# A wait for the landing of the third gather ahead, in the edge stage of a graph-attention and mixture-of-experts kernel

## The chip, the core and the metric

The kernel runs on one core of a Trainium2 chip. The metric is the device time of one execution in microseconds (us), lower is better. A core has TensorE (PE, its weight loads are listed apart as PEld), VectorE (DVE), ScalarE (ACT), GpSimd (POOL) and SyncE (SP), which run their own instruction streams and meet at semaphores, and 16 DMA engines that move data between the core's memory and HBM.

## The reference, cut to what matters

The program is a graph layer followed by an expert layer. The change touches the edge part of the graph layer alone:

```python
feat_all = einsum('ni,rhid->rnhd', layernorm(x), conv_weights)      # 8 relations, 4 heads of 64
feat_src_e = feat_all[edge_type, edge_src]                          # one row per edge, 120000 edges
feat_dst_e = feat_all[edge_type, edge_dst]
el = sum(feat_src_e * attn_l[edge_type], -1); er = sum(feat_dst_e * attn_r[edge_type], -1)
e = leaky_relu(el + er, 0.2)
alpha = softmax of e over the edges of one destination node
h = segment_sum(alpha[..., None] * feat_src_e, edge_dst, 3750)      # 3750 nodes x 256
x = x + h + h_bias
x = x + top2_of_8_experts_ffn(layernorm(x))
```

All of it is float32.

## The kernel before, in words

There are three stages, one after the other. `node_stage` normalizes the 3750 node rows, multiplies them with the weights of all relations and stores `feats` in HBM: a row of `FW` = 260 words (256 features and 4 left logits) for each node and relation. `edge_stage` walks over the edges. `route_expert_stage` picks two experts for each node and computes them.

The edges are sorted by destination. 256 consecutive edges are a block of two units of 128 edges (one edge to a partition); a pair is a block together with one tile of 128 destination nodes, and there are 498 pairs. They are taken in 32 groups (`SIZES`: 8 pairs, then 30 groups of 16, then 10). A full group has `GU` = 32 units. The rows of `feats` that a group's edges read are fetched by the 32 gathers of line 798: each is one indirect DMA issued on POOL, which reads an index from each of 128 partitions and brings 128 rows of 260 words (133 KB) into `gath[:, r, u]`. There are `GBUFS` = 3 buffers `r`, taken in turn by the groups, and 996 gathers in all.

What sets the order is written out by hand: every engine has a function `period(g, r, n)`, run in a loop of three groups per turn by `each_period` (line 732 is its loop). In the words of one group `g`:

* POOL (`gather_features`, from line 786): waits until the index columns of its group are there (`idx_ready`), and for each quad `j` of four units until the buffer is free. A buffer is free quad by quad as PE finishes the sums of the group three before (`sum_ready`, value `freed(g, j)`). The waits go through `wait_apart` (lines 158 and 159), an instruction of its own that waits and then counts up an unused semaphore. In the program a wait stands once per four gathers, and the four gathers follow it without a wait. The gathers of groups 0 to 2 wait for nothing.
* DVE: scales the gathered rows by alpha (line 905), adds PE's sums to `acc` (line 914), computes the softmax shifts, and at the end of `period(g)` the logits of the next group (`logits`, line 838), which is the first reader of the gathered rows of group `g + 1`. It waits for one semaphore of the buffer, `gath_in[r]`, to reach the count of all gathers so far into this buffer (`landed`). A gather adds 16 to it when its data has landed.
* ACT: builds one-hot matrices of destinations (lines 1035, 1038), copies their transposes (`hotT`, line 1045), takes the exponentials (lines 1073 to 1075) and scales two quads of a group (line 1063).
* PE: transposes the one-hots (line 1113), looks up the right logits (line 1138), and sums the scaled rows (line 1154).
* SP: loads the edge records (line 183) four groups ahead, and at the end, when all gathers have landed, loads the node rows (line 784).

In the program gathers run ahead of their use: while PE sums the first quads of group `g`, POOL gathers group `g + 3`, and the logits that come next are those of group `g + 1`.

Of the kernel before, what the change touches and what calls it, by code (L numbers as in the profile page):

```python
# [44 lines left out]
BLK = 2  # L45
# [3 lines left out]
GB = 16  # L49
GU = GB * BLK  # L50
assert GU * HEADS == P
SIZES = [8] + [GB] * ((PAIRS - 18) // GB) + [10]
SHORT = GB - SIZES[0]
# [7 lines left out]
GBUFS = 3  # L61
# [93 lines left out]
def wait_apart(pool, sem, value, carrier):  # L155


    pool.wait_ge(sem, value)
    pool.sem_inc(carrier, 1)
# [14 lines left out]
def load_records(nc, sp, sb, edges, meta, g, landed, of=range(GB)):  # L174

    edge_rows = edges.rearrange("t h c e -> (t h) (c e)")
    for b in of:
        if b % 4 == 0:
            starts = nc.values_load_multi_w_load_instructions(
                sb["pair_row"][0:1, bass.ds(g, 1), b:b + 4].rearrange("a g b -> a (g b)"), engines=(mybir.EngineType.SP,),  # L180
                min_val=0, max_val=(CHUNK_ROWS - BLK) * HEADS)[1]
        at = starts[b % 4]
        sp.dma_start(meta[b * BLK * HEADS:(b + 1) * BLK * HEADS], edge_rows[bass.ds(at, BLK * HEADS), :]).then_inc(landed, 16)
# [441 lines left out]
def edge_stage(nc, sb, edges, feats, xb, wr, br):  # L625
# [6 lines left out]
    with ExitStack() as ctx:  # L632
# [6 lines left out]
        def sem(name):  # L639
            return ctx.enter_context(nc.semaphore(name))  # L640
# [9 lines left out]
        reset, cat, idxT, ndlT, typeT = sb["reset"], sb["cat"], sb["idxT"], sb["ndlT"], sb["typeT"]  # L650
# [24 lines left out]
        SLOTS_Q = GU // QUAD  # L675
        LAG = 3
        PQ = QUAD // BLK

        meta_in = sem("meta_in")
        gath_in = [sem(f"gath_in{r}") for r in range(GBUFS)]  # L680
        rows_ready, rowsT_ready, idx_ready = sem("rows_ready"), sem("rowsT_ready"), sem("idx_ready")
        hot_ready, hotT_ready, hotT_copied, er_done = sem("hot_ready"), sem("hotT_ready"), sem("hotT_copied"), sem("er_done")
        e_ready, eT_ready, spread_ready, lv_ready = sem("e_ready"), sem("eT_ready"), sem("spread_ready"), sem("lv_ready")
# [5 lines left out]
        carrier = sem("carrier")  # L689

        def quads(g):

            if not isinstance(g, int):
                return SLOTS_Q
            return SIZES[g] // PQ if 0 <= g < GROUPS else 0

        def pairs_before(g):
            return BASES[g] if isinstance(g, int) else g * GB - SHORT

        def quads_before(g):  # L700
            return BASES[g] // PQ if isinstance(g, int) else g * SLOTS_Q - SHORT // PQ

# [4 lines left out]
        def landed(g, r, n):  # L707

            if isinstance(g, int):
                return 16 * BLK * sum(SIZES[r:g + 1:GBUFS])  # L710
            return 16 * BLK * GB * (n + 1) - (16 * BLK * SHORT if r == 0 else 0)

        def freed(g, j):

            if isinstance(g, int):
                return BASES[g - GBUFS] + min(PQ * j + PQ, SIZES[g - GBUFS])
            return pairs_before(g - GBUFS) + PQ * j + PQ

        def tiles_of(engine, g, j, n):

            numbers = pair_tile[0:1, bass.ds(g, 1), PQ * j:PQ * (j + n)].rearrange("a g b -> a (g b)")
            return nc.values_load_multi_w_load_instructions(
# [3 lines left out]
        def each_period(eng, body, first, last_loop):  # L726


            for g in range(first):
                body(g, g % GBUFS, g // GBUFS)  # L730
            loops = (last_loop + 1 - first) // GBUFS
            with eng.Fori(0, loops) as i:
                for k in range(first, first + GBUFS):
                    body(i * GBUFS + k, k % GBUFS, i + k // GBUFS)
            for g in range(first + GBUFS * loops, GROUPS + 1):
                body(g, g % GBUFS, g // GBUFS)

        def there(g):
            return not isinstance(g, int) or 0 <= g < GROUPS

        LAST_LOOP = GROUPS - 4
        LAST, LAST2 = GROUPS - 1, GROUPS - 2
        ACT_SCALES = [(LAST2, j) for j in range(3, SIZES[LAST2] // PQ)] + [(LAST, j) for j in range(2, SIZES[LAST] // PQ, 2)]
        ACT_Q = (6, 7)
# [21 lines left out]
        with nc.Block() as block:  # L766
            @block.sync
            def _(sp):
                load_records(nc, sp, sb, edges, meta, AHEAD, meta_in)

                def period(g, r, n):
                    if there(g + AHEAD + 1):
                        sp.wait_ge(rows_ready, g + 1)
                        load_records(nc, sp, sb, edges, meta, g + AHEAD + 1, meta_in)

                each_period(sp, period, 2, GROUPS - AHEAD - 2)
                sp.dma_start(sb["wr_sb"][:], wr.rearrange("(k p) e -> p k e", p=P)).then_inc(sb["small_in"], 16)
                sp.dma_start(sb["br_all"][:], br.to_broadcast([P, EXPERTS])).then_inc(sb["small_in"], 16)

                sp.wait_ge(sum_ready, BASES[LAST2])  # L780
                sp.wait_ge(gath_in[LAST % GBUFS], landed(LAST, LAST % GBUFS, 0))
                x_tiles = xb.rearrange("(t p) f -> p t f", p=P)
                for b, (lo, hi) in enumerate(BATCHES_R):
                    sp.dma_start(rows_of_nodes(sb)[:, lo:hi], x_tiles[:, lo:hi]).then_inc(sb["x_in"][b], 16)

            @block.gpsimd
            def _(pool):
                def gather_features(g, r, n):
                    if not there(g):
                        return  # L790
                    if not isinstance(g, int) or g >= AHEAD:
                        wait_apart(pool, idx_ready, g - (AHEAD - 1), carrier)
                    for j in range(quads(g)):
                        if not isinstance(g, int) or g >= GBUFS:

                            wait_apart(pool, sum_ready, freed(g, j), carrier)
                        for u in range(j * QUAD, (j + 1) * QUAD):
                            pool.indirect_dma_start(gath[:, r, u], None, feats,  # L798
                                                    bass.IndirectOffsetOnAxis(ap=idxT[:, r, u:u + 1], axis=0)).then_inc(gath_in[r], 16)

                each_period(pool, gather_features, GBUFS + 1, GROUPS - 2)

            @block.vector
            def _(dve):
# [28 lines left out]
                def logits(g, r, n):  # L833

                    dve.wait_ge(picked, g * 2 + 2)
                    dve.wait_ge(gath_in[r], landed(g, r, n))
                    e0 = e_sb[:, 0].rearrange("p (u h) -> p u h", h=HEADS)
                    step(dve.tensor_tensor(e0, gath[:, r, :, D:FW], er_e[:], ALU.add))
                    dve.scalar_tensor_tensor(e_sb[:, 1], e_sb[:, 0], SLOPE, e_sb[:, 0], ALU.mult, ALU.max).then_inc(e_ready, 1)
# [123 lines left out]
                def period(g, r, n):  # L963
# [53 lines left out]
                    if there(g + 1):  # L1017
                        logits(g + 1, rn, n if r < GBUFS - 1 else n + 1)
# [216 lines left out]
def rows_of_nodes(sb):  # L1235

    words = sb["gath"][:, NODE_BUF].rearrange("p u w -> p (u w)")
    return words[:, 0:TILES * D].rearrange("p (t d) -> p t d", t=TILES)
# [737 lines left out]
def build(nc, ins, out):  # L1976
# [3 lines left out]
    with ExitStack() as ctx:  # L1980
        def keep(name, shape, dt=F32):
            return ctx.enter_context(nc.sbuf_tensor(name, shape, dt))

        sb = {
            "cst": keep("cst", [P, C_W]),
            "er": keep("er", [P, TILES, RELS * HEADS]),
            "acc": keep("acc", [P, TILES, FW]),
            "tile_of": keep("tile_of", [P, GROUPS]),
            "tile_off": keep("tile_off", [P, GROUPS]),
            "pair_tile": keep("pair_tile", [1, GROUPS, GB], I32),  # L1990
            "pair_row": keep("pair_row", [1, GROUPS, GB], I32),
            "reset": keep("reset", [P, GBUFS, UNIT + 1]),
            "cat": keep("cat", [P, GBUFS, 5]),
            "idxT": keep("idxT", [P, GBUFS, GU], I32),
            "ndlT": keep("ndlT", [P, GBUFS, GU]),
            "wr_sb": keep("wr_sb", [P, KD, EXPERTS]),
            "br_all": keep("br_all", [P, EXPERTS]),
            "typeT": keep("typeT", [P, GBUFS, GU, RELS]),
        }
        node_stage(nc, sb, ins["x"], ins["conv"], ins["conv_t"], ins["attn"], ins["attn_rows"], ins["edges"], ins["numbers"], feats, slots_x,  # L2000
                   ins["consts"], ins["bias"], xb)
        sb["gath"] = keep("gath", [P, GBUFS, GU, FW])
        sb["small_in"] = ctx.enter_context(nc.semaphore("small_in"))
        sb["x_in"] = [ctx.enter_context(nc.semaphore(f"x_in_r{b}")) for b in range(len(BATCHES_R))]
        edge_stage(nc, sb, ins["edges"], feats, xb, ins["wr"], ins["br"])
        route_expert_stage(nc, sb, ins["experts1"], ins["experts2"], ins["b2"], slots_x, out)
# [48 lines left out]
```

## Time and profile before

| what | value |
| --- | --- |
| runs, three of them | 2082.37, 2082.75 and 2084.45 us, median 2082.75 us |
| profiled execution | span 2456.4 us; its own time is not given beside the span |
| granted TensorE clock over the span | 0.813 of full speed |
| busy, share of the span | PE 77%, PEld 65%, DVE 43%, ACT 44%, POOL 46% |
| gathers of line 798 | 996, 950.6 us busy |
| DMA | 315.51 MB, of which the queue of POOL's DMAs 149.24 MB |

The profiled execution is 373.65 us longer than the median of the runs. The views used are: busy time by stretch (its last columns are the granted TensorE clock, the DMA engines' mean busy share and what they moved), groups of instructions, the list of waits, the list of instructions in order of time, and the view of one line with who waited for it. Starts are from the beginning of the span. In a list in order of time the columns are the start, how long, engine, line, operation, what it writes and reads, and in brackets how long the engine was idle before and what ended that. "issue" is idle time that ended without a releaser that the profile shows, "remote" an unknown releaser.

### The profile page before, as it was taken

The numbers are of one execution on the slowest core, as the hardware profiler recorded it, in microseconds if no ns is written. First come the engines' busy times: TensorE is split into PE (matmuls) and PEld (weight loads), VectorE is DVE, ScalarE is ACT, GpSimd is POOL, SyncE is SP. The second block draws the span as 40 slices with busy tenths as digits, with TensorE's granted clock in tenths as the row PEclk, the third lists the DMA queues.
The fourth block names the chain that finished last, engine by engine and source line by source line (L and its number), as shares of the span: only waits on it lengthen the run. The fifth ranks groups of instructions, "written<-read, shape, count | busy, mean of one in ns | idle before, by whom it ended". The sixth has DMA issues, their size and how long they took to land. (4 is left out here: it accounts for less than half of the span.)

```text
span 2456.4 us, 35279 instructions
## 1 busy us (share of the span) xinstructions
PE 1898.8 (77%) x9138; PEld 1594.8 (65%) x9139; DVE 1062.3 (43%) x3018; ACT 1076.9 (44%) x3259; POOL 1142.0 (46%) x1164
## 2 busy tenths in 40 slices
PE   8999125767767777867777777677877689999998
PEld 7887124656655665656565666565665668999887
DVE  6332013545555555545555555455567532221111
ACT  2222123645555545554555555454656532222221
POOL 4000744556666566666666566656620443122222
PEclk9999556787877768777787777777788689999999
DMA  6443422333333333333333333333312877777774
GB/s 239 189 170 143 109 67 74 84 90 88 90 92 92 88 88 91 90 88 90 88 92 92 89 90 90 92 85 88 91 44 80 282 230 221 248 246 247 241 234 104
DMA packets 121157, 315.51 MB, mean 128 GB/s; under 512 B 27047, under 2 KB 71335, under 8 KB 106180
## 3 DMA queue, kind: packets, MB, share of 16 engines
q0 software_dynamic: 60192, 149.24, 23.4%
q1 hardware_dynamic: 60836, 164.88, 19.3%
q8 instruction: 41, 0.67, 0.1%
q14 instruction: 88, 0.72, 0.1%
HBM read 257.36 MB, written 57.71 MB: 128 GB/s over the span
## 5 line engine op out<-in xcount | busy, mean ns | idle before, releaser
L798 POOL DMA_INDIRECT gath<-feats,idxT x996 | 950.6, 954 | 799.1 <-issue 272.7
L1154 PE MATMUL psP<-gath,hot 128*128 128x260 f32 x1992 | 668.1, 493 | 28.6 <-DVE gath L905 15.1
L1154 PEld LDWEIGHTS psP<-gath,hot 128*128 128x128 f32 x1992 | 469.4, 247 | 123.5 <-issue 35.4
L1113 PE MATMUL psOT<-cst,hot 128*128 128x128 f32 x996 | 196.1, 331 | 346.0 <-ACT hotT L1045 231.9
L1045 ACT COPY hotT<-psOT 128x512 f32<-128x512 f32 x249 | 143.5, 576 | 628.6 <-remote 485.4
L1113 PEld LDWEIGHTS psOT<-cst,hot 128*128 128x128 f32 x996 | 139.7, 171 | 407.2 <-issue 309.0
L1138 PEld LDWEIGHTS psE<-er,hotT 128*128 128x128 f32 x1992 | 309.7, 235 | 48.6 <-issue 44.9
L914 DVE TENSOR_TENSOR acc<-acc,psP 128x260 f32 x498 | 211.0, 424 | 295.3 <-remote 127.9
L1138 PE MATMUL psE<-er,hotT 128*128 x1992 | 309.5, 305 | 31.1 <-issue 19.9
L1035 ACT ACTIVATE hot<-cst,ndlT 128x128 f32<-128x128 f32 x996 | 316.2, 391 | 4.7 <-PEq L325 4.7
L1680 ACT ACTIVATE acc<-psH,w1buf 128x256 f32<-128x256 f32 (+1 forms) x344 | 122.4, 423 | 346.7 <-PE psH L1571 304.3
L1063 ACT ACTIVATE gath<-gath 128x64 f32<-128x64 f32 x1040 | 261.0, 337 | 0.1
L1496 POOL DMA_INDIRECT out<-acc,node x66 | 103.3, 1565 | 335.0 <-DVE acc L1904 178.0
L1571 PE MATMUL psH<-acc,w1buf 128*128 128x256 f32 (+1 forms) x1376 | 241.9, 334 | 4.4 <-issue 2.4
L1587 PE MATMUL psY<-w2buf,acc 128*128 128x256 f32 x1056 | 240.9, 384 | 3.4 <-issue 3.3
L905 DVE TENSOR_TENSOR gath<-gath,psA 128x1024 f32<-128x1024 f32 x184 | 224.5, 1221 | 27.2 <-ACT gath L1075 19.9
L1571 PEld LDWEIGHTS psH<-acc,w1buf 128*128 128x128 f32 x1376 | 217.8, 194 | 24.8 <-DVE acc L1888 2.9
L585 PE MATMUL psF<-wext,xT 128*128 128x264 f32 x960 | 221.1, 388 | 1.1 <-ACT xT L536 1.1
L1587 PEld LDWEIGHTS psY<-w2buf,acc 128*128 128x128 f32 x1056 | 200.0, 193 | 32.4 <-issue 6.8
L585 PEld LDWEIGHTS psF<-wext,xT 128*128 128x128 f32 x960 | 180.7, 191 | 31.6 <-ACT xT L536 1.5
L1038 ACT ACTIVATE hot<-hot 128x512 f32<-128x512 f32 x249 | 156.8, 630 | 38.3 <-remote 25.9
L1888 DVE TENSOR_SCALAR acc<-psX,w1buf 128x256 f32<-128x256 f32 (+1 forms) x86 | 37.5, 478 | 214.8 <-PE psX L1556 186.1
(232 smaller groups left out, 1178.5 us busy)
## 6 DMA issues: line engine op xcount, KB each, us to landing
w1buf<-in_experts SPq DMA_DIRECT2D x43, 1030.0 KB
w2buf<-in_experts SPq DMA_DIRECT2D x43, 1024.0 KB
feats<-frow SPq DMA_DIRECT2D x29, 1040.0 KB, 3.9
gath<-feats,idxT POOLq DMA_INDIRECT x996
meta<-in_edges SPq DMA_DIRECT2D x464, 12.0 KB
acc<-slots_x SPq DMA_DIRECT2D x23, 258.0 KB
gath<-in_b SPq DMA_DIRECT2D x43, 128.0 KB
acc<-slots_x SPq DMA_DIRECT2D x20, 129.0 KB
```

Of the source, the lines that this page charges most:

```text
L585: ins = pe.matmul(psF[:, n % BUFS, j, 0:W], xT[:, i % LEAD, k], wext[:, k, 2 * pair + j], start=k == 0, stop=k == KD - 1)
L798: pool.indirect_dma_start(gath[:, r, u], None, feats, bass.IndirectOffsetOnAxis(ap=idxT[:, r, u:u + 1], axis=0)).then_inc(gath_in[r], 16)
L905: dve.tensor_tensor(feat, feat, alpha.unsqueeze(3).to_broadcast([P, QUAD, HEADS, HD]), ALU.mult).then_inc(scaled, 1)
L914: dve.tensor_tensor(into[b % PQ], into[b % PQ], psP[:, bank(g, b, r), 0:FW], ALU.add).then_inc(sum_used, 1)
L1035: ins = act.activation(hot[:, r, u], iota, ACT.Square, bias=ndlT[:, r, u:u + 1])
L1038: act.activation(hot[:, r, j * QUAD:(j + 1) * QUAD], hot[:, r, j * QUAD:(j + 1) * QUAD], ACT.Relu, bias=1.0, scale=-1.0).then_inc(hot_read ...
L1063: ins = act.activation(feat, feat, ACT.Copy, scale=gath[:, r, u, D + h:D + h + 1])
L1113: ins = pe.transpose(psOT[:, k * P:(k + 1) * P], hot[:, r, j * QUAD + k], ident)
L1138: ins = pe.matmul(psE[:, u * W % 512:u * W % 512 + W], hotT[:, j % 2, k * P:(k + 1) * P], tables[k // BLK], start=True, stop=True)
L1154: ins = pe.matmul(psP[:, bank(g, b, r), 0:FW], hot[:, r, u], gath[:, r, u], start=u % BLK == 0, stop=u % BLK == BLK - 1)
L1571: ins = pe.matmul(psH[:, bank(n, g), at * slots(n):(at + 1) * slots(n)], w1(n, k, m), xeT[:, n % 2, k, 0:slots(n)], start=k == 0, stop=k = ...
L1587: ins = pe.matmul(psY[:, y_bank(n, j), 0:D], hT[:, n % 2, m, j * P:(j + 1) * P], w2(n, m), start=m == 0, stop=m == KH - 1)
```

## The change

Each buffer gets four semaphores in place of one, and its gathers add to them in turn (`u % TURNS`). From the fourth unit of a group on (`u >= FLYING`), a gather first waits until the third gather ahead of it in the same buffer has landed, again through `wait_apart`. DVE's logits and SP's load at the end wait for all four semaphores of the buffer. The count of a semaphore in a buffer's turn is worked out by `landed` and the new `landed_before`. The first three gathers of a group get no new wait. That makes 29 new waits in each of the 30 full groups, 13 in the first and 17 in the last: 900 in all. Nothing else is changed; from here on, line numbers in the changed program are larger by 8 to 14.

```diff
+        FLYING = 3
+        TURNS = 4
 
-        gath_in = [sem(f"gath_in{r}") for r in range(GBUFS)]
+        gath_in = [[sem(f"gath_in{r}_{q}") for q in range(TURNS)] for r in range(GBUFS)]
...
         def landed(g, r, n):
 
             if isinstance(g, int):
-                return 16 * BLK * sum(SIZES[r:g + 1:GBUFS])
-            return 16 * BLK * GB * (n + 1) - (16 * BLK * SHORT if r == 0 else 0)
+                return 16 * sum(SIZES[r:g + 1:GBUFS]) * BLK // TURNS
+            return 16 * GB * BLK // TURNS * (n + 1) - (16 * SHORT * BLK // TURNS if r == 0 else 0)
+
+        def landed_before(g, r, n):
+
+            if isinstance(g, int):
+                return 16 * sum(SIZES[r:g:GBUFS]) * BLK // TURNS
+            return 16 * GB * BLK // TURNS * n - (16 * SHORT * BLK // TURNS if r == 0 else 0)
...
                 sp.wait_ge(sum_ready, BASES[LAST2])
-                sp.wait_ge(gath_in[LAST % GBUFS], landed(LAST, LAST % GBUFS, 0))
+                for q in range(TURNS):
+                    sp.wait_ge(gath_in[LAST % GBUFS][q], landed(LAST, LAST % GBUFS, 0))
...
                         for u in range(j * QUAD, (j + 1) * QUAD):
+                            if u >= FLYING:
+
+                                wait_apart(pool, gath_in[r][(u - FLYING) % TURNS], landed_before(g, r, n) + 16 * ((u - FLYING) // TURNS + 1), carrier)
                             pool.indirect_dma_start(gath[:, r, u], None, feats,
-                                                    bass.IndirectOffsetOnAxis(ap=idxT[:, r, u:u + 1], axis=0)).then_inc(gath_in[r], 16)
+                                                    bass.IndirectOffsetOnAxis(ap=idxT[:, r, u:u + 1], axis=0)).then_inc(
+                                                        gath_in[r][u % TURNS], 16)
...
                     dve.wait_ge(picked, g * 2 + 2)
-                    dve.wait_ge(gath_in[r], landed(g, r, n))
+                    for q in range(TURNS):
+                        dve.wait_ge(gath_in[r][q], landed(g, r, n))
```

The order of POOL's instructions at the start of the loop's first group, before. `gath` is the buffer, `feats` the rows in HBM, `idxT` the indices; in brackets are the semaphores that an instruction, or a waiting instruction ahead of it, waits for.

```order
L158 ISA [waits idx_ready]
L798 DMA gath<-feats,idxT 128x260 [waits sum_ready]
L798 DMA gath<-feats,idxT 128x260 x3
L158 REGISTER_ALU
L798 DMA gath<-feats,idxT 128x260 [waits sum_ready]
```

The same place in the changed program:

```order
L158 ISA [waits idx_ready]
L810 DMA gath<-feats,idxT 128x260 [waits sum_ready]
L810 DMA gath<-feats,idxT 128x260 x2
L158 ISA
L810 DMA gath<-feats,idxT 128x260 [waits gath_in1_0]
L158 REGISTER_ALU
L810 DMA gath<-feats,idxT 128x260 [waits sum_ready,gath_in1_1]
L810 DMA gath<-feats,idxT 128x260 [waits gath_in1_2]
L810 DMA gath<-feats,idxT 128x260 [waits gath_in1_3]
```

The gathers keep their order; every gather from the fourth on has a wait of its own ahead of it, the first of a quad two.

The end of a group on DVE, before, and then changed. `er_e` holds the right logits, `e_sb` the sum of both:

```order
L905 TENSOR_TENSOR gath<-gath,psA 128x4x256 [waits sum_used]
L838 TENSOR_TENSOR e_sb<-gath,er_e 128x128 [waits gath_in1,picked]
L839 SCALAR_TENSOR_TENSOR e_sb<-e_sb 128x128 [waits v_step_edges]
```

```order
L919 TENSOR_TENSOR gath<-gath,psA 128x4x256 [waits sum_used]
L852 TENSOR_TENSOR e_sb<-gath,er_e 128x128 [waits gath_in1_2,gath_in1_1,gath_in1_3,gath_in1_0,picked]
L853 SCALAR_TENSOR_TENSOR e_sb<-e_sb 128x128 [waits v_step_edges]
```

The logits stand where they stood, right behind the scaling of a quad, and wait for four semaphores of the buffer in place of one.

## Rows read from the trace of the kernel before

**Rows 1.** Busy time by stage: stretch, length, engines, clock, DMA share, GB/s.

```profile
0.00:243.00 243.00, 228.70 (x1049) 193.19 (x1050) 92.43 (x251) 55.97 (x171) 27.64 (x35) 1.00 0.50 187
378.00:1881.00 1503.00, 1110.84 (x5164) 901.34 (x5163) 796.20 (x2161) 813.21 (x2545) 874.14 (x916) 0.77 0.33 88
1881.00:2456.00 575.00, 522.59 (x2771) 466.83 (x2769) 158.11 (x551) 174.28 (x458) 163.80 (x133) 0.93 0.70 221
```

**Rows 2.** The gathers as a line: duration in ns min/median/max, first and last start.

```profile
L798 POOL DMA_INDIRECT gath<-feats,idxT x996: 947/953/1144, 243.6 to 1806.6; - x200
```

**Rows 3.** The list of waits: in total us, times, longest.

```profile
ACT hotT L1045 <- remote: 485.4, 66, 50.3
...
POOL gath L798 <- issue: 272.7, 860, 1.7
...
POOL gath L798 <- PE psP L1154: 204.7, 83, 34.3
...
DVE acc L914 <- remote: 127.9, 53, 7.2
POOL gath L798 <- remote: 121.8, 46, 3.3
```

**Rows 4.** POOL in order of time, one group of the loop.

```profile
1007.95 0.95 POOL L798 DMA_INDIRECT gath<-feats,idxT  x1 [1.73 <-PE psP L1154]
1009.21 0.96 POOL L798 DMA_INDIRECT gath<-feats,idxT  x1 [0.30 <-issue]
...
1038.58 0.95 POOL L798 DMA_INDIRECT gath<-feats,idxT  x1 [0.30 <-issue]
...
1047.38 0.95 POOL L798 DMA_INDIRECT gath<-feats,idxT  x1 [0.31 <-issue]
```

**Rows 5.** Busy time by half microsecond behind the last gather of a run.

```profile
344.50:345.00 0.50, 0.00 (x0) 0.00 (x0) 0.00 (x0) 0.00 (x0) 0.00 (x0) 0.50 0.57 108
345.00:345.50 0.50, 0.00 (x0) 0.00 (x0) 0.00 (x0) 0.00 (x0) 0.00 (x0) 0.50 0.44 158
345.50:346.00 0.50, 0.00 (x0) 0.00 (x0) 0.00 (x0) 0.00 (x0) 0.00 (x0) 0.50 0.00 0
```

**Rows 6.** POOL in order of time, that last gather and the next one.

```profile
343.12 0.95 POOL L798 DMA_INDIRECT gath<-feats,idxT  x1 [0.30 <-issue]
378.38 0.95 POOL L798 DMA_INDIRECT gath<-feats,idxT  x1 [34.31 <-PE psP L1154]
```

**Rows 7.** PE in order of time, the sums that free a quad.

```profile
1003.70 3.39 PE L1154 MATMUL psP<-gath,hot 128*128 128x260 f32 x8
```

**Rows 8.** DVE in order of time, the end of a group.

```profile
1036.46 0.42 DVE L914 TENSOR_TENSOR acc<-acc,psP 128x260 f32 x1 [0.23 <-issue]
1036.91 1.22 DVE L905 TENSOR_TENSOR gath<-gath,psA 128x1024 f32<-128x1024 f32 x1
1038.05 0.28 DVE L838 TENSOR_TENSOR e_sb<-gath,er_e 128x128 f32<-128x128 f32 x1
```

**Rows 9.** The logits as a line: what its engine sat idle for.

```profile
L838 DVE TENSOR_TENSOR e_sb<-gath,er_e x32: 284/284/359, 312.6 to 1857.5; 128x128 f32<-128x128 f32 x32
its engine sat idle before it (us, times) until:
  issue: 0.2, 1
```

**Rows 10.** PE and ACT in order of time, a pause inside a run of gathers.

```profile
1038.91 0.65 PE L1113 MATMUL psOT<-cst,hot 128*128 128x128 f32 x4
...
1040.76 0.63 ACT L1038 ACTIVATE hot<-hot 128x512 f32<-128x512 f32 x1
...
1050.58 0.58 ACT L1045 COPY hotT<-psOT 128x512 f32<-128x512 f32 x1 [9.19 <-remote]
```

**Rows 11.** POOL in order of time, in the expert stage: a DMA behind another one's landing.

```profile
2130.30 1.57 POOL L1496 DMA_INDIRECT out<-acc,node  x1 [0.31 <-issue]
2140.13 1.55 POOL L1496 DMA_INDIRECT out<-acc,node  x1 [8.27 <-DMA out<-acc,node]
```

## The prediction

> **What bounds the kernel now.** I read the stages first, since the change touches one of them. The node stage and the expert stage keep PE busy for 94% and 91% of their time [rows 1]. In the 1503.0 us between them, the edge stage, PE is busy 74%, at a granted clock of 0.77, and no engine is full. The gathers are spread over nearly all of it: 996, the first at 243.6 us, the last at 1806.6 [rows 2], so 1563.0 us for 995 steps from one gather's start to the next, 1.571 us each. Then the list of waits: POOL waits 204.7 us in 83 places for PE's sums, that is for free buffers, and 121.8 us in 46 for an unknown releaser [rows 3]. Where it waits for nothing, from 1038.58 to 1047.38, seven steps take 8.80 us, 1.257 us each: 0.95 of work and 0.30 that the view calls issue [rows 4]. 995 steps of that would take 1250.7 us, so POOL had 312.3 us to spare in this execution. Nobody waits for the gathers either: before the 32 logits, their first reader, DVE idled 0.2 us in all, and not for a landing [rows 9]. The cause is the lead of more than a group that the gathers have. In the profiled execution POOL is therefore covered.
>
> It need not be covered in the runs. They are 373.65 us shorter (2456.4 against 2082.75). If the time outside the gathers' stretch is what the trace shows, 2456.4 - 1563.0 = 893.4 us, then 2082.75 - 893.4 = 1189.4 us are left for the 995 steps, 1.195 us each. That is below the 1.257 us of the trace's free pace. So in the runs either the rest is at least 61 us shorter as well, or a step is shorter than 1.257; either way the gathers are close to being what the edge stage waits for, and what slows them counts nearly in full. That is why a change on an engine that is 46% busy has to be costed with care. The sum below is made against the 2456.4 us span and carried over to the median of the runs unchanged, with the reserve worked out at both paces.
>
> **The change part by part.**
>
> The 900 new waits on POOL. A gather `u` can start when gather `u - 3` has landed, the increment has reached POOL, and POOL has handed on the gather. Landing: the last gather of a run starts at 343.12 and no other follows until 378.38 [rows 6]; the DMA engines are busy 57% and 44% in the two half microseconds up to 345.50 and not at all in the next [rows 5]. So its packets, those that count up the semaphore among them, end at most 2.38 us after its start. With steps of 1.257 us, the gather before is then 3.64 us old: two gathers are in flight, never three, and the limit is not reached. From release to start: PE's sums end at 1003.70 + 3.39 = 1007.09 [rows 7] and the gather that waited for them starts at 1007.95 [rows 4], 0.86 us, with the way of that semaphore in it. The round trip is 2.38 + 0.86 = 3.24 us. What it has to fit into is three steps: 3.77 us at 1.257, or 3.59 us at 1.195. The reserve is 0.53 or 0.35 us. The trace of before has no gather that waits for a landing. The round trip has a lower bound in 1.88 + 0.86 = 2.74 us, if the packets ended right behind 345.00. An upper one is 3.74 us: another half microsecond, one step of that view, for a DMA's increment to reach POOL. Farther away is one wait for a landing, in the expert stage: from the start of a DMA at 2130.30 to the start of the next at 2140.13, 9.83 us [rows 11]. It adds into rows in HBM, its work alone takes 1.57 us against 0.95, and the gather's packets were seen to end; I leave it out of the range. At 3.74 us the trace's own pace still costs nothing, and the pace of 1.195 would grow to 3.74 / 3 = 1.247, or 0.052 x 900 = 47 us. I take 3.24 us, since both parts are measured on this queue, and so a cost of 0, and 1 us for single late landings. The range keeps 0 and 47.
>
> A page of the Trainium skill bears on the piece that I could not see. DMA: Bandwidth & Descriptors, in "Anatomy of one DMA — SWDGE (gpsimd) path", puts the semaphore update at about 100 ns once the write's receipt is in, and most of the fixed 2 us before it. By the page the round trip would be about 3.34 us and the sum 0 at either pace; by my upper row bound it would be 47 us at the faster one. No row here shows that piece by itself.
>
> The wait instructions themselves. A quad already has one, and behind it the second gather starts at the usual 0.30 us [rows 4]. POOL's instruction stream runs ahead of the descriptor work, so a wait that is satisfied lies beside the 0.95 us of the gather before: 0. If that cover is gone, the gather starts 0.86 us after its release; that is in the round trip already. Behind a waiting POOL stand only further gathers; who waits for those is DVE's logits.
>
> DVE: three more semaphores at the logits, 32 times. A wait between two dependent adds shows 0.23 us of idle [rows 8]. Two more of these would be 0.46 x 32 = 14.7 us without cover. But the logits at 1038.05 start before the scaling ahead of them (1036.91 + 1.22 = 1038.13) is over [rows 8], so the waits are passed during it: 0. If the landings came late, only the last of the four would be waited for, and the other three would be through. SP: three more waits, once, ahead of the load of the node rows, at most 3 x 0.23 = 0.7 us, not counted fully. Fewer queued gathers could also help a transfer that shares the DMA engines; these are busy 33% in the stage [rows 1], so nothing is taken for it.
>
> The sum is 0 + 1 + 0 + 0.3 = 1.3 us, or 2082.75 + 1.3 = **2084 us**. 0.2% (4.2 us) is about what a measurement can tell from no change, so this is no change.
>
> **The rivals.**
>
> *The round trip decides the pace (slower).* Place: POOL's wait between a gather and the third one ahead. It decides as soon as three steps of the runs are shorter than the round trip; at 3.24 us that is a step under 1.08 us, at 3.74 one under 1.247. For it: the 1.195 us above, and that nothing of the 0.30 us of issue is explained, so that a step of the runs may be shorter still. Against it: the reserve at 3.24. Halfway, at 3.6 us to 3.7, a step of 1.20 to 1.23 comes out, and the 900 waits cost 0.005 to 0.038 us each, 5 to 34 us; with 20 us the time is 2103 us. If POOL is slack in the runs too, the first part of it is absorbed.
>
> *Gather runs hold up the others, and the wait breaks them (faster).* In the trace ACT has nothing to do from 1041.39 (1040.76 + 0.63) to 1050.58, while PE's transposes for its copy were through at 1039.56 [rows 10]; the pause ends some three microseconds after POOL's run of gathers ended at 1047.38 [rows 4]. Such pauses before the copy sum to 485.4 us [rows 3]. For it: the coincidence, and 127.9 us more of the kind on DVE. Against it: the runs are 373.65 us shorter, so most of these pauses are not in them; and a limit that is never reached breaks no run. If the limit did bite and a tenth of the 485.4 us stood in the runs and half of it went, the gain would be 24 us: 2058 us.
>
> *The waits are not free on the streams (slower, small).* If DVE's cover fails, 14.7 us, and the time is 2098 us. Against it: the overlap in rows 8, and that the logits never waited.
>
> That the change does nothing at all is my forecast's own mechanism: two in flight where three are allowed, and the first three gathers of a group are not held at all, as the order shows.
>
> **How the numbers follow.** No change in effect, 2084 us: 50%, because every row puts the round trip below three steps. The round trip or its late cases decide: 32%. The waits on the streams: 7%. Fewer pauses: 11%. Within 0.2% I put 0.49; slower 0.40, the two slower rivals and a point of the forecast's own tail; faster 0.11. The range runs from 2076 us, where a small gain is still in, to 2115 us; beyond it lie most of the faster rival (its 24 us) and the part of the first rival near 47 us and above, together 2 in 10. The forecast's own range is 2080 to 2088.
>
> **What would show it.** Right: in the stretches where POOL waits for no sums, the step from gather to gather is 1.26 us still, and the list of waits has no or only short waits of POOL for a landing; the logits still start beside the scaling ahead of them. The first rival would show as steps of a third of the round trip, and POOL's idle time ended by the landing of `gath`. The second as shorter pauses of ACT before the copy of `hotT`. The forecast is wrong if the runs differ from 2082.75 by more than 4.2 us, and its reason is wrong if POOL's free step grows beyond 1.30 us.

## The result, and the profile after

The changed kernel takes 2117.91 us (median of four runs, 2117.03 to 2123.70), the kernel before 2083.36 us: a ratio of 1.0167, 95% interval 1.0151 to 1.0182, so 34.6 us **slower**. The forecast was no change, 2084 us, and its range ended at 2115.

The profiled execution of the changed kernel has a span of 2116.2 us, which is its time in the runs. That of the kernel before had 2456.4, and its run times were 373 us shorter. So before anything is compared, the kernel before was run and profiled once more, unchanged, as one of the experiments. That execution has a span of 2086.4 us. The first profile, on which the prediction rests, had caught an execution that no timed run resembles. From here on "the second profile of before" is the one that the changed kernel is compared with; where a row answers to one of the first, its group is named.

The line of the gathers, in the second profile of before (it answers to [rows 2]; below it, what POOL idled for ahead of them, and who waited for them):

```profile
L798 POOL DMA_INDIRECT gath<-feats,idxT x996: 949/953/1197, 244.4 to 1499.0; - x200
its engine sat idle before it (us, times) until:
  issue: 293.5, 963
...
  PE psP L1154: 9.8, 32
who waited for it (us, times):
  DVE e_sb L838: 176.3, 31
```

The same view of the changed kernel:

```profile
L810 POOL DMA_INDIRECT gath<-feats,idxT x996: 947/953/1167, 244.5 to 1534.2; - x200
its engine sat idle before it (us, times) until:
  issue: 307.2, 937
...
  DMA gath<-feats,idxT: 21.9, 25
  PE psP L1168: 10.4, 33
who waited for it (us, times):
  DVE e_sb L852: 213.0, 31
  POOL gath L810: 44.3, 38
...
DMA to landing us min/median/max: 2.7/2.8/3.8
```

Three readings. First, the gathers set the pace of the edge stage already in the kernel before. From the first to the last start it is 1254.6 us for 995 steps, 1.261 us each, hardly more than the free step of 1.257 [rows 4]; POOL idles 9.8 us for PE's sums, in 32 places and so no longer than the usual 0.3 us each, where the first profile had 204.7 us [rows 3]; and DVE waits 176.3 us for landings ahead of its logits, in 31 of 32 places, where the first profile had 0.2 us in all [rows 9]. Second, the whole loss lies between the gathers: 1289.7 us in place of 1254.6 is 35.1 us, against 34.6 of the runs; behind the start of the last gather nothing is lost, 582.0 us against 587.4. Third, it is not spread over the 900 waits. 25 of them ended with a landing that POOL was idle for, 21.9 us, and the idle time called issue is 13.7 us more. Nearly all other steps are still 1.26 us.

POOL in order of time shows the two kinds of gap in the changed kernel. Two windows with the first kind:

```profile
864.30 0.95 POOL L810 DMA_INDIRECT gath<-feats,idxT  x1 [0.30 <-issue]
866.89 0.95 POOL L810 DMA_INDIRECT gath<-feats,idxT  x1 [1.64 <-issue]
868.15 0.95 POOL L810 DMA_INDIRECT gath<-feats,idxT  x1 [0.30 <-issue]
...
946.99 0.96 POOL L810 DMA_INDIRECT gath<-feats,idxT  x1 [0.30 <-issue]
950.00 0.95 POOL L810 DMA_INDIRECT gath<-feats,idxT  x1 [2.05 <-issue]
```

And the second kind, from two other windows:

```profile
415.71 0.95 POOL L810 DMA_INDIRECT gath<-feats,idxT  x1 [0.30 <-issue]
418.69 0.95 POOL L810 DMA_INDIRECT gath<-feats,idxT  x1 [2.02 <-DMA gath<-feats,idxT]
...
1486.18 0.95 POOL L810 DMA_INDIRECT gath<-feats,idxT  x1 [0.30 <-issue]
1488.12 1.05 POOL L810 DMA_INDIRECT gath<-feats,idxT  x1 [0.99 <-DMA gath<-feats,idxT]
```

*Pauses 64 gathers apart.* Counted from the first gather, the gaps at 866.89 and 950.00 are at numbers 478 and 542. They recur at 606, 670 and so on to 990, and at 222 to 414 ahead of these: 13 in a strict step of 64, and one at 159. A gap adds 1.29 to 1.75 us, 19.7 us in all 14. In POOL's own instruction stream (the records of waits and register work, which the list in order of time leaves out) the trace shows a pause at these places: at gather 606, which starts at 1032.03, its own wait is over at 1029.68, and the next record of the stream comes at 1031.82, 2.1 us later, where elsewhere it comes after some 0.5 us. *Late landings.* The 62 other gaps of over 0.04 us sum to 18.4 us. Of the 15 over 0.3 us, 12 stand three places behind a gather whose last packet ended 2.8 to 3.4 us after its start, by the packets of POOL's queue, where the median is 2.45. The new waits don't make such packets: in both profiles of before single gathers have their last packet up to 3.3 and 3.4 us after their start, too. Together the gaps are 38.1 us over 995 steps of 1.257; the second profile of before has 3.3 us of them. The difference is 34.8 us, where the runs differ by 34.6.

That leaves a theory and two rivals, which the expectations call by letters. **A, a reserve that is too thin**: the gathers set the pace; a queue of gathers ahead of POOL's descriptor work had covered both kinds of irregularity, and a wait for the third gather ahead leaves too little of it. **B**: the wait instructions themselves cost, on POOL or in DVE's logits. The other rival is that the gathers are covered, as the first profile shows, and the loss arises elsewhere.

### The profile page after: what moved, and what is told of

Read it like the earlier page. It is cut to its first block and busy times, and to the rows that moved or that the text cites. A ratio compares the mean times of both kernels' runs of the same rounds, so it can differ in the third digit from the quotient of the medians.

```text
span 2116.2 us, 36357 instructions
## 1 busy us (share of the span) xinstructions
PE 1771.1 (84%) x9138; PEld 1518.1 (72%) x9139; DVE 1058.9 (50%) x3018; ACT 1077.5 (51%) x3259; POOL 1142.7 (54%) x1164
## 5 line engine op out<-in xcount | busy, mean ns | idle before, releaser
L1168 PE MATMUL psP<-gath,hot 128*128 128x260 f32 x1992 | 585.5, 445 | 2.9 <-DVE gath L919 1.9
L1168 PEld LDWEIGHTS psP<-gath,hot 128*128 128x128 f32 x1992 | 417.8, 220 | 71.4 <-DVE gath L919 3.7
L1152 PEld LDWEIGHTS psE<-er,hotT 128*128 128x128 f32 x1992 | 292.6, 224 | 28.8 <-issue 26.7
L1152 PE MATMUL psE<-er,hotT 128*128 x1992 | 291.3, 295 | 15.5 <-DVE er_e L842 15.4
L1127 PE MATMUL psOT<-cst,hot 128*128 128x128 f32 x996 | 189.6, 323 | 45.6 <-ACT hotT L1059 40.0
L1233 PE MATMUL psS<-cst,e_sb 128*128 128x128 f32 x31 | 14.6, 470 | 197.6 <-DVE e_sb L853 197.6
```

Of the source, the lines that this page charges most:

```text
L1127: ins = pe.transpose(psOT[:, k * P:(k + 1) * P], hot[:, r, j * QUAD + k], ident)
L1152: ins = pe.matmul(psE[:, u * W % 512:u * W % 512 + W], hotT[:, j % 2, k * P:(k + 1) * P], tables[k // BLK], start=True, stop=True)
L1168: ins = pe.matmul(psP[:, bank(g, b, r), 0:FW], hot[:, r, u], gath[:, r, u], start=u % BLK == 0, stop=u % BLK == BLK - 1)
```

## The experiments

All but the last two start from the changed kernel. The kernel before was measured again beside them; its median was 2083.36 us beside the changed kernel, 2084.57 us beside the first four experiments and 2086.35 us beside the last four. So each result is read by its ratio to the runs of before that stand beside it; the ratio given is not exactly that of the two medians.

**Four in flight.**

```diff
-        FLYING = 3
+        FLYING = 4
```

> Theory A (a reserve that is too thin): in the kernel before, the edge stage goes at the pace of the gathers, 1.257 us each, and with three in flight a gather's way from start to landing (2.45 us) and from there to the start of the gather that waits for it (1.25 us at least) is 3.70 us of the 3.77 us that three steps last, so that a late landing or a pause of POOL's instruction stream is lost time: 38 us of it in the trace of the changed kernel. With FLYING = 4 the reserve is 5.03 - 3.70 = 1.33 us, more than all late landings (up to 3.43 us, so 0.98 late) and nearly all of the pauses (1.35 to 1.75): 2083 to 2088 us. Theory B (the wait instructions themselves cost, on POOL or in DVE's logits): 869 waits instead of 900, so 2116 to 2118 us.

Measured: 2085.87 us, ratio to before 1.0011 (1.0002 to 1.0021). The first gather starts at 243.5, the last at 1498.8, 1255.3 us:

```profile
L810 POOL DMA_INDIRECT gath<-feats,idxT x996: 947/953/1159, 243.5 to 1498.8; - x200
its engine sat idle before it (us, times) until:
  issue: 287.0, 937
...
  DMA gath<-feats,idxT: 2.7, 9
```

Waits for a landing still end an idle time in 9 places, but for 2.7 us in all. The pause is still in POOL's stream (at gather 606 its own wait and the next one end at 1005.54 and 1007.70, 2.16 us apart), and this gather starts only 0.13 us late. One step more of reserve takes back all but about 2 us (0.4 to 4.4 by the interval). B falls: 868 waits (the expectation says 869) cost no more than that.

**The same waits, for landings long past.**

```diff
-                            if u >= FLYING:
+                            if u >= FLYING and (not isinstance(g, int) or g >= GBUFS):
 
-                                wait_apart(pool, gath_in[r][(u - FLYING) % TURNS], landed_before(g, r, n) + 16 * ((u - FLYING) // TURNS + 1), carrier)
+                                wait_apart(pool, gath_in[r][(u - FLYING) % TURNS], landed_before(g, r, n), carrier)
```

> The same wait instructions from group 3 on, at the same places and on the same semaphores, but for a value that was reached when the buffer was filled the time before, so that no landing holds a gather. Theory A: 2082 to 2086 us. Theory B: 2110 us and more, since 829 of the 900 wait instructions are still there.

Measured: 2085.98 us, ratio 1.0003 (0.9992 to 1.0015). An instruction that waits for nothing is free here. It is what the wait waits for that costs. The list of waits (in all, times, longest, in us), for the changed kernel and then for this one:

```profile
POOL gath L810 <- issue: 307.2, 937, 2.1
...
POOL gath L810 <- issue: 291.7, 957, 0.3
```

This run also shows the cover itself. In POOL's instruction stream the wait of a gather is over 15.3 us (median) before that gather starts, so the stream is 12 gathers ahead; in the changed kernel it is over 0.96 us before. And the pauses are there in both: with the settled waits, at the same 14 gathers, 159, 222, 286 and so on to 990, the next wait ends 2.15 to 2.29 us behind the gather's own, while the gathers themselves start with no gap. In the second profile of before the stream is 15.3 us ahead at the waits of the quads as well.

**A hole in the waits.**

```diff
-                            if u >= FLYING:
+                            if u >= FLYING and not 8 <= u < 16:
```

> FLYING = 3, but gathers 8 to 15 of a group have no wait. 14 of the gaps in the trace of the changed kernel, 19.7 us, stand at gather 14 or 15 of every second group, 64 gathers apart; other gaps at gathers 8 to 15 sum to 4.2 us, gaps elsewhere to 14.2 us. Theory A with both kinds of gap: about 24 us less, 2094 us (2090 to 2098). If late landings alone cost the time and the gaps 64 apart cost nothing in the end: 2110 us or more. Theory B (waits cost, 232 fewer of 900): 2109 us.

Measured: 2093.44 us, ratio 1.0042 (1.0029 to 1.0055), 8.8 us above before. The 256 waits that are gone here (the expectation says 232), 28% of the 900, carried three quarters of the loss. The sum of the gaps had 24 of 38 us at them.

```profile
L810 POOL DMA_INDIRECT gath<-feats,idxT x996: 947/953/1144, 244.3 to 1507.8; - x200
its engine sat idle before it (us, times) until:
  issue: 290.1, 938
...
  DMA gath<-feats,idxT: 10.1, 14
```

The issue time is nearly back at the level of four in flight, with a longest of 0.6 us; what is left is 10.1 us behind late landings.

**Four semaphores alone.** `FLYING = 99`, so that no gather waits for a landing, while DVE and SP wait for all four semaphores.

> No new wait on POOL, but four semaphores per buffer, with DVE and SP waiting for all four. Theory A: 2082 to 2085 us. If DVE's additional waits cost (0.46 us in 32 places at most): up to 2098 us.

Measured: 2086.66 us, 1.7 us above the upper end of what theory A was to give, ratio 1.0008 (0.9997 to 1.0018). By the ratio, DVE's three additional semaphores cost nothing that can be told from none, although DVE now does stand at this place and wait.

**The complement of the hole.**

```diff
-                            if u >= FLYING:
+                            if 8 <= u < 16:
```

> The complement of the hole: only gathers 8 to 15 of a group wait for the third one ahead (248 or so of the 900 waits). Theory A with both kinds of gap: the gaps 64 apart (19.7 us in the trace of the changed kernel) and the 4.2 us of others at these gathers remain, the rest goes: about 2084 + 24 = 2108 us (2103 to 2110). If all waits cost alike (34.5 us over 900): 2094 us.

Measured: 2108.04 us, ratio 1.0108 (1.009 to 1.0125), 22.5 us above before (21.7 by the medians). 256 waits are left here. The pauses are at the same gathers as in the changed kernel, 159, 222, 286 and so on to 990, and in the list of waits (in all, times, longest, in us) the idle time called issue carries them:

```profile
POOL gath L810 <- issue: 311.6, 956, 2.3
```

The two halves add up to 8.8 + 22.5 = 31.3 us of 34.6, which is all of it within the intervals. So the loss is made gather by gather, at the places where the gaps are. The kernels that wait at 900, 868, 829 and 256 gathers have their pauses at the same gathers, so the pauses go by the count of gathers, not by that of POOL's waits.

**Two in flight.**

```diff
-        FLYING = 3
+        FLYING = 2
```

> FLYING = 2: each gather waits for the landing of the second one ahead. Theory A with a round trip of 3.70 us: two gathers per 3.70 us from the third of a group on, 58.0 us per full group in place of 40.2, times 996 / 32 = 31.1 is 554 us more, and some 20 us for late landings and pauses: 2640 to 2680 us. With the round trip of 3.24 us of the prediction: (3.24 / 2 - 1.257) x 931 = 338 us more, 2422 us. Theory B (instructions): 2120 us.

Measured, one run: 2619.84 us, 20 us under the lower end of what was expected. POOL in order of time, in the middle of the stage:

```profile
1012.19 0.95 POOL L810 DMA_INDIRECT gath<-feats,idxT  x1 [0.75 <-DMA gath<-feats,idxT]
1014.02 0.95 POOL L810 DMA_INDIRECT gath<-feats,idxT  x1 [0.87 <-DMA gath<-feats,idxT]
1015.73 0.95 POOL L810 DMA_INDIRECT gath<-feats,idxT  x1 [0.75 <-DMA gath<-feats,idxT]
```

Here the wait decides at most gathers (a landing ends the idle time in 542 places), and the round trip can be read off: from 1012.19 to 1015.73 it is 3.54 us for two. That is the 2.8 us from start to landing of the line's view, and some 0.75 us from the landing to the start of the gather that waited. (The 0.75 in the brackets is another thing, the idle time behind the gather before. In POOL's stream a wait is over 0.74 us, the median, before its gather starts.) The 3.70 us of my expectation was 0.15 too long: in the changed kernel the wait is over 0.96 us before the start, since POOL is still at the gather before. The pauses and late landings of this run are in its time, too. With three in flight the reserve is then 3.77 - 3.55 = 0.22 us.

**Three of four gathers.** This one starts from the kernel before. Its expectation says what is left out.

```diff
-                return 16 * BLK * sum(SIZES[r:g + 1:GBUFS])
-            return 16 * BLK * GB * (n + 1) - (16 * BLK * SHORT if r == 0 else 0)
+                return 16 * sum(BLK * SIZES[k] * (4 if k <= GBUFS else 3) // 4 for k in range(r, g + 1, GBUFS))
+            return 16 * (24 * (n - 1) + 48 if r == 0 else 24 * n + 32)
...
+                            if u % QUAD == QUAD - 1 and (not isinstance(g, int) or g > GBUFS):
+                                continue
                             pool.indirect_dma_start(gath[:, r, u], None, feats,
```

> The kernel before, but from group 4 on the last gather of each quad is left out (221 of 996, 278 us of steps of 1.257 us); the rows of an earlier group stand in its place, the rest of the computation is unchanged. Theory A (the gathers set the pace of the edge stage): 130 to 200 us less, 1885 to 1950 us, as far as the 184 us that DVE waits for landings before its logits when no new wait stands on POOL; then another engine is the bound. If the gathers are covered, as the profile of the kernel before shows them: 2080 us or more.

Measured, one run: 1919.53 us, 167 us under the kernel before (median 2086.35 us beside it). DVE's wait for landings is gone but for 30.7 us, and POOL now waits for free buffers and indices:

```profile
L800 POOL DMA_INDIRECT gath<-feats,idxT x775: 950/957/1183, 243.8 to 1292.2; - x194
its engine sat idle before it (us, times) until:
  issue: 214.3, 687
...
  PE psP L1156: 67.3, 71
  DVE ndlT L216: 25.5, 16
who waited for it (us, times):
  DVE e_sb L840: 30.7, 4
```

So the gathers do set the pace, and the next bound lies some 160 us below. Part of where it lies is the clock: between 500 and 1292 us the granted clock was 0.97 of full speed in this run and 0.85 in the second profile of before.

**The kernel before, again.**

> The kernel before, unchanged, for a second profile. If its first profile (a span of 2456 us, ACT and SP held up for microseconds inside runs of gathers, POOL waiting for free buffers) was a matter of that one profiled execution: a span near 2083 us, with DVE waiting for landings. If the profiler does it to this kernel every time: a span near 2456 us again, while the times stay at 2083 us.

Measured: a time of 2088.27 us with a span of 2086.4, whose line of the gathers is shown above. The profiler doesn't stretch this kernel as such: every profile but the first has a span within 3 us of its kernel's median time. What held that one execution up isn't known. No version that does all of the gathers is faster than the kernel before.

## Why the prediction was wrong

*"So in the runs either the rest is at least 61 us shorter as well, or a step is shorter than 1.257."* The first branch holds: outside the gathers' stretch the second profile of before has 2086.4 - 1254.6 = 831.8 us, 61.6 us less than the 893.4 of the first. The usual step is 1.26 us in every run in which no landing decides. That the gathers are close to being what the edge stage waits for, and that what slows them counts nearly in full, was right, against what the profile showed by itself. One reading in front of it was loose: the 1503.0 us are not all that lies between the two other stages. The row starts at 378 us, and the 135 us from 243 us on, in which POOL waited 34.3 us for a free buffer, belong to the edge stage too. The forecast doesn't use it.

*The round trip, 3.24 us, with a reserve of 0.53 or 0.35.* It is 3.55 us and the reserve 0.22. The landing was right as far as packets go (at most 2.38, median 2.45), but what POOL waits for comes later: 2.8 us after the start. The Trainium skill, DMA: Bandwidth & Descriptors, "Anatomy of one DMA — SWDGE (gpsimd) path", gives about 0.1 us for the semaphore update once the write's receipt is in. Here 2.8 - 2.45, some 0.35 us, lie between the last packet and the landing, and no row tells how much of that is the receipt. The way from release to start is 0.75 us, where I had 0.86 from a wait for PE. "Two gathers are in flight, never three" doesn't hold either: two steps are 2.51 us, and the landing comes at 2.8, so for 0.3 us of each step three are on their way. Even so the median gather fits: a fixed round trip of 3.55 would have cost nothing.

*"And so a cost of 0, and 1 us for single late landings."* **This is the step that failed.** I priced the wait by the gather that lands on time, and took its distance from the limit for safety. With a reserve of 0.22 us nearly all of what is irregular is lost, and it is 35 us: by the sums of the gaps about 20 in pauses of POOL's stream and 15 in late landings. The hole (8.8 us without the pauses' gathers) and its complement (22.5 us) agree with that. The late landings could have been seen: packets up to 3.3 us after the start stand in the first profile of before. The pauses leave no gap between the gathers of before.

*"POOL's instruction stream runs ahead of the descriptor work, so a wait that is satisfied lies beside the 0.95 us of the gather before: 0."* Right for an instruction whose condition is old (2085.98 us with 829 of them, and the stream 15.3 us ahead). But I named this cover and didn't ask what else lay under it. A wait for the third gather ahead keeps the stream from running farther ahead than the landing allows, and a pause of 2.1 us in it then shows with 1.33 us and more. "If that cover is gone, the gather starts 0.86 us after its release" priced the usual gather again.

*DVE and SP at 0.3 us together:* right, within what four semaphores alone can tell (2086.66 us).

*The first rival, "the round trip decides the pace", 5 to 34 us, at 32%.* The sign, the place and nearly the size; of the mechanism only what "or its late cases" says beside the 32%, for 15 of the 35 us, and nothing of the pauses. As it was priced it wanted steps of a third of the round trip everywhere, and the steps stayed at 1.26 us with some 30 large gaps. That its 5 to 34 us come near the 34.6 measured is luck: they are worked out from a step of 1.195 us, which no run has. My test, "the reason is wrong if POOL's free step grows beyond 1.30 us", would have passed it by: the mean step grew to 1.296 us, the usual one not at all. The range left out the upper part of this rival, and that is where the time fell.

*The faster rival.* The pauses of ACT on which it rested [rows 10], with an unknown releaser, are in none of the later profiles; they were part of the one odd execution. ACT still waits before this copy, 290.2 us in the second profile of before, but for PE's transposes.

## What to carry to other kernels

Where the limited transfers set the pace, the reserve of a limit on what is in flight has to cover the worst round trip and the longest pause of the issuing engine, not the median: here 0.22 us of reserve cost 34.6 us, and with one step more, 1.48 us, it was about 2. An issuing engine that is 46% busy in the profile can still be the one that sets the pace: the step from start to start times their number (1.257 x 995 = 1250.7 us) is to be laid against what the real runs leave for that stage. And where the profiled execution differs from the runs by 18%, it is to be taken again before its waits are read; its durations held (0.95, 0.30, 2.45 us), but its waits did not, nor did its picture of which engines are covered.

## What the runs showed of the hardware that was not expected

* POOL's instruction stream pauses for about 2.1 us once in 64 gathers (at 222, 286 and so on to 990 in the changed kernel, with four in flight, with the settled waits and in the complement of the hole). Where the stream runs 15.3 us ahead, as with the settled waits, no gather starts late by it. What it does there isn't settled; no kernel was run for it.
* A gather of 128 rows of 1040 bytes has its last packet 2.45 us after its start (median) and its landing 2.8 us after it (2.7 to 3.8 in the changed kernel, up to 4.8 with two in flight), and a gather that waits for that starts 0.75 us later.
* One profiled execution of a kernel took 2456 us and a second one 2086.
